# A selective-scan decoder block on one core: in the five quads without X tiles, TensorE sums the third sequence's shared products in a kept PSUM bank

## The chip, the cores and the metric

One NeuronCore of a Trainium2 chip runs the whole program. The metric is the device time of one execution in microseconds (us). The kernel before takes 2988.18 us, the median of 3 runs (2986.87 to 2988.26).

## What is computed

Input `x` is 16 sequences of 128 tokens and 1024 features, all float32. Three residual layers follow one another, each closed by a layer norm. Only the first matters here, a Mamba-like block:

```
proj = x @ W_in.T;  x, gate = proj[:, :2048], proj[:, 2048:]
x    = silu(causal_conv4(x))                      # u
ts, B, C = rms parts of x @ W_x.T                 # 64, 16, 16 columns
dt   = softplus(ts @ W_dt.T + b_dt);  A = -exp(A_log)
state[d, n] = state[d, n] * exp(dt[d] * A[d, n]) + dt[d] * u[d] * B[n]   # over time
y[d] = sum over n of state[d, n] * C[n]           # n = 0..15
out  = ((y + u * D) * silu(gate)) @ W_out.T
```

The sum over `n`, the 16 indices of the state, is what the change touches.

## The kernel before, in words

Tokens are cut into 4 groups of 4 sequences (512 tokens), the 2048 channels into 16 tiles of 128. A **quad** is 4 channel tiles of one group; 16 quads (s = 0 to 15, four to a group) run one after another, and each goes through the 16 indices n. One index of one quad is called a **step** below.

What a step does, engine by engine:

- ScalarE (ACT) writes exp(dt*A) of each of the 4 tiles into banks 0 and 1 (L1168).
- GpSimd (POOL) makes dt*u*B for all 4 tiles in one instruction (L1346).
- VectorE (DVE) scans each tile over time (L1433, 4 a step). It does so two steps ahead: during step n it scans for n+2.
- TensorE (PE) transposes the scanned states, so that tokens lie on partitions, one **turn** of 4 transposes for each sequence b = 0 to 3, into bank 2 (b even) or 3 (b odd) (L620). A turn waits until its bank has been read.
- The product with C[n] and the sum over n: sequences 0, 1 and 2 are done by DVE in one instruction each, `acc = bank * C + acc` (`dve_acc`, L1449, or L1445 for the first index). Sequence 3 (`OWN`) is multiplied by ACT (`act_part`, L912) and added by POOL (`pool_sums`, L1277). The third sequence, b = 2, called `SPLIT`, is divided: for the indices in `SHARED` = (0, 3, 6, 9, 12) ACT multiplies (`act_part2`, L926) and POOL adds into `acc2` (`pool_sums2`, L1285); for the other 11 DVE does it.

Between the turns PE works through **filler**: matmuls of 128x512 that make the Z tiles (gate, 8 products each, L526), the X tiles (conv input, 8 each, also L526), the D tiles (dt, 1 each, L538) and the O tiles (output projection of the quad before, 4 each, L550). `ORDER` fixes their order and `SIZES` how many come in the first and the second half of a step: turns 0 and 1, filler, turns 2 and 3, filler. X tiles are made ahead and are finished with quad 10 (`has_x`), so in quads 11 to 15 their places in the order are empty. Quads 11 and 15 are the last of their group and follow the fourth row of `ORDER`; 12, 13 and 14 follow the other.

At the end of a quad PE waits for the sums, turns them back (4 **Y** tiles, L661 to L664, where a matmul by the identity adds `acc2` to the third sequence), and DVE adds u*D (L1558) and multiplies by the gate (L1568, which counts up `fin`).

All X, Z, D, O and Y tiles live in banks 4 to 7, handed out in turn: `home` is bank 4 + k % 4 for the k-th of them, and `pe_room` waits until the tile four places earlier has been read (`FREED`).

Of the kernel before, what the change touches and what calls it, by code (L numbers as in the profile page):

```python
# [33 lines left out]
QD = 4  # L34
# [18 lines left out]
SPLIT = OWN - 1  # L53
SHARED = (0, 3, 6, 9, 12)
KEPT = OWN * N - len(SHARED)


LEAD = 5 * QD
EARLY = DT + 2
HEAD = 4  # L60
OPENING = "X-2 X-1 Z0 X0 D0 Z1 X1 D1 D2 Z2 D3 X2 Z3 X3".split()
# [34 lines left out]
def kept(s, n, b):  # L96

    return KEPT * s + OWN * n - sum(v < n for v in SHARED) + b + 1 - (b == SPLIT and n in SHARED)


def shared(s, n):

    return len(SHARED) * s + sum(v <= n for v in SHARED)

# [9 lines left out]
JOBS = jobs()  # L114
PLACE = {j: k for k, j in enumerate(JOBS)}
TILES = [j for j in JOBS if j[0] in "XZ"]
# [16 lines left out]
def program(nc, a, out):  # L133
# [4 lines left out]
    with ExitStack() as ctx:  # L138
# [100 lines left out]
        def home(kind, i):  # L239
            return bank(4 + PLACE[kind, i] % 4)  # L240

# [341 lines left out]
        def pe_filler(pe, s, p):  # L583
# [18 lines left out]
            assert start == sum(sizes)  # L602

        def pe_step(pe, s):
            g, q = divmod(s, NQ)
            for n in range(N):
                U = N * s + n

                def turn(b):

                    if b == 1:
                        after(pe, "part_ok", U)
                    elif b > 1:
                        pe.wait_ge(S["acc_ok"], kept(s, n, b - 2))
                    elif U and (n - 1) % N in SHARED:
# [37 lines left out]

            pe.wait_ge(S["acc_ok"], KEPT * (s + 1))
# [260 lines left out]
        def act_part2(act, s, n):  # L915

            k = SHARED.index(n)
            act.wait_ge(S["t_done"], QD * (N * s + n) + SPLIT + 1)
            if k == 0:
                after(act, "yt_mm", QD * s)  # L920
                act.wait_ge(S["cg_ok"], s // NQ + 1)
                dst = acc2
            else:
                after(act, "sum2_ok", (len(SHARED) - 1) * s + k - 2)
                dst = part2[:, k % 2, :]
# [3 lines left out]
        def act_opening(act, n, slot):  # L929
# [229 lines left out]
        def act_step(act, s):  # L1159
            q = s % NQ  # L1160
            for n in range(N):
# [10 lines left out]
                if U >= 2:  # L1172
                    if (U - 2) % N in SHARED:
                        act_part2(act, (U - 2) // N, (U - 2) % N)
                    act_part(act, (U - 2) // N, (U - 2) % N)

        def act_keys(act, b, o):
# [101 lines left out]
        def pool_sums2(pool, s, n):  # L1279
            k = SHARED.index(n)  # L1280
            if k == 0:
                return
            pool.wait_ge(S["part2_ok"], shared(s, n))
            after(pool, "sum2_ok", (len(SHARED) - 1) * s + k - 1)
            nc.gpsimd.tensor_tensor(acc2, acc2, part2[:, k % 2, :], ALU.add).then_inc(S["sum2_ok"], 1)  # L1285
# [18 lines left out]
        def pool_step(pool, s):  # L1304
# [9 lines left out]
            for n in range(N):  # L1314
# [121 lines left out]
        def dve_acc(dve, s, n, b):  # L1436
# [9 lines left out]
            else:  # L1446
                before = n - 2 if b == SPLIT and n - 1 in SHARED else n - 1
                dve.wait_ge(S["acc_ok"], kept(s, before, b))
# [84 lines left out]
        def dve_step(dve, s):  # L1533
            if s % NQ == 0:
                after(dve, "acc_ok", KEPT * s)
                after(dve, "part_ok", N * s)
                after(dve, "part2_ok", len(SHARED) * s)
                if s > 0:
                    dve_c(dve)
            for n in range(N):  # L1540
                U = N * s + n

                for part in range(2):
                    for b in range(2 * part, min(2 * part + 2, OWN)):
                        if b != SPLIT or n not in SHARED:
                            dve_acc(dve, s, n, b)
# [306 lines left out]
        def _(pool):  # L1853
# [138 lines left out]
```

## Time and profile before

| | |
|---|---|
| median of 3 runs | 2988.18 us |
| the profiled execution | 2988.28 us, its span 2986.3 us |
| busy PE / DVE / POOL / ACT | 2728.6 / 2563.8 / 1918.7 / 1694.1 us |
| quad 10, the last with X tiles | 126.4 us |
| quads 11, 12, 13, 14, 15 | 124.3, 118.5, 124.3, 118.2, 114.0 us |
| the rest after quad 15 | 774.6 us, which the change does not touch |

A quad is taken here from the last Y turn of one to the last Y turn of the next. The clock column of the windows view is the mean clock granted to TensorE, 1.00 being 2.4 GHz; the two levels are 1.2 and 2.4 GHz. A busy PE includes matmuls that overlap their neighbours, so start-to-start times are used for prices. Each float32 product of 128x512 is two MATMUL records, each transpose one.

### The profile page before, as it was taken

The numbers are of one execution on the slowest core, as the hardware profiler recorded it, in microseconds if no ns is written. First come the engines' busy times: TensorE is split into PE (matmuls) and PEld (weight loads), VectorE is DVE, ScalarE is ACT, GpSimd is POOL, SyncE is SP. The second block draws the span as 40 slices with busy tenths as digits, with TensorE's granted clock in tenths as the row PEclk, the third lists the DMA queues.
The fourth block names the chain that finished last, engine by engine and source line by source line (L and its number), as shares of the span: only waits on it lengthen the run. The fifth ranks groups of instructions, "written<-read, shape, count | busy, mean of one in ns | idle before, by whom it ended". The sixth has DMA issues, their size and how long they took to land.

```text
span 2986.3 us, 35300 instructions
## 1 busy us (share of the span) xinstructions
PE 2728.6 (91%) x11120; PEld 1559.2 (52%) x11120; DVE 2563.8 (86%) x3529; ACT 1694.1 (57%) x2848; POOL 1918.7 (64%) x885
## 2 busy tenths in 40 slices
PE   8978899999989999998999888788889999999996
PEld 4445555555555555555555455455544555555553
DVE  2389999999999999999999999999966787787785
ACT  2356566575656656565565655656534555555553
POOL 1159897888969888896988988889841222222221
PEclk9989899999999999999999999899999999999998
DMA  4443333534243343424333322322401211111110
GB/s 155 144 109 88 97 93 101 144 91 135 84 153 99 108 138 86 137 85 158 93 107 101 100 87 78 132 84 68 117 29 37 98 56 56 63 56 56 63 58 27
DMA packets 132876, 281.32 MB, mean 94 GB/s; under 512 B 12528, under 2 KB 12656, under 8 KB 132224
## 3 DMA queue, kind: packets, MB, share of 16 engines
q1 hardware_dynamic: 132736, 279.59, 31.3%
q8 instruction: 72, 1.18, 0.2%
q14 instruction: 68, 0.56, 0.1%
HBM read 245.86 MB, written 33.69 MB: 94 GB/s over the span
## 4 chain that ended last, share of the span: by engine, by line
PE 53%; DVE 32%; issue 8%; ACT 5%; DMA 1%; POOL 1%; DVEq 0%; SPq 0%; ACTq 0%; POOLq 0%
DVE arena L1433 17%; PE banks L526 14%; PE banks L550 9%; DVE arena L1449 7%; PE banks L620 7%; PE banks L766 4%; PE banks L719 3%; PE banks L675 3%; PE banks L700 3%; PE banks L563 2%; PE banks L730 2%; PE banks L690 2%; DVE arena L1378 2%; ACT banks L1168 1%; PE banks L773 1%
## 5 line engine op out<-in xcount | busy, mean ns | idle before, releaser
L1346 POOL TENSOR_TENSOR arena<-arena 128x2048 f32<-128x2048 f32 x254 | 1153.9, 4543 | 78.3 <-PE banks L620 78.3
L1433 DVE TENSOR_TENSOR_SCAN arena<-banks,arena 128x512 f32<-128x512 f32 x1024 | 1185.1, 1203 | 13.5 <-POOL arena L1346 7.5
L1168 ACT ACTIVATE banks<-arena,a_sb 128x508 f32<-128x508 f32 x1024 | 696.9, 684 | 734.5 <-DVE arena L1433 731.0
L526 PE MATMUL banks<-arena 128*128 128x512 f32 x2048 | 954.0, 603 | 11.5 <-DMA arena<-in_xT 8.2
L620 PEld LDWEIGHTS banks<-ident,arena 128*128 128x128 f32 x4096 | 492.6, 146 | 406.8 <-issue 176.6
L620 PE MATMUL banks<-ident,arena 128*128 128x128 f32 x4096 | 574.3, 284 | 127.9 <-DVE arena L1449 66.5
L526 PEld LDWEIGHTS banks<-arena 128*128 128x128 f32 x2048 | 373.1, 195 | 363.0 <-issue 358.2
L1449 DVE SCALAR_TENSOR_TENSOR arena<-banks,cg,arena 128x512 f32<-128x512 f32 x640 | 452.6, 737 | 74.9 <-PE banks L620 74.1
L550 PE MATMUL banks<-arena 128*128 128x512 f32 x1024 | 470.5, 598 | 5.5 <-DMA arena<-in_WoutT 4.2
L1277 POOL TENSOR_TENSOR arena<-arena 128x512 f32<-128x512 f32 x240 | 306.4, 1277 | 210.1 <-ACT arena L912 207.6
L1359 POOL TENSOR_TENSOR arena<-arena 128x512 f32<-128x512 f32 x128 | 141.3, 1104 | 433.0 <-DVE arena L1614 432.9
L550 PEld LDWEIGHTS banks<-arena 128*128 128x128 f32 x1024 | 185.9, 193 | 187.4 <-issue 185.2
L1378 DVE SCALAR_TENSOR_TENSOR arena<-banks,taps,arena 128x508 f32<-128x508 f32 (+2 forms) x192 | 141.6, 737 | 102.8 <-ACT arena L821 98.3
L912 ACT ACTIVATE arena<-banks,cg 128x512 f32<-128x512 f32 x256 | 171.9, 671 | 13.2 <-PE banks L620 13.2
L1200 ACT ACTIVATE arena<-arena 128x512 f32<-128x512 f32 x128 | 80.7, 630 | 172.2 <-DVE arena L1603 171.9
L1289 POOL TENSOR_TENSOR arena<-arena 128x512 f32<-128x512 f32 x64 | 81.9, 1280 | 133.2 <-ACT arena L835 133.2
L1599 DVE TENSOR_REDUCE arena<-banks 128x8 f32<-128x512 f32 x128 | 88.2, 689 | 87.8 <-PE banks L719 87.7
L719 PE MATMUL banks<-arena 128*128 128x512 f32 x256 | 131.7, 596 | 1.3 <-DVE rbuf L1462 1.3
L1368 POOL TENSOR_TENSOR ve<-ve,mhalf 128x1 f32<-128x1 f32 x32 | 17.4, 542 | 174.4 <-DVE ve L1646 174.4
L700 PE MATMUL banks<-arena 128*128 128x512 f32 x256 | 122.9, 592 | 0.0
L675 PE MATMUL banks<-arena 128*128 128x512 f32 x256 | 120.5, 593 | 1.7 <-ACT arena L1182 1.7
L766 PE MATMUL banks<-arena 128*128 128x512 f32 x256 | 115.1, 593 | 0.7 <-ACT arena L1208 0.7
(140 smaller groups left out, 2987.2 us busy)
## 6 DMA issues: line engine op xcount, KB each, us to landing
arena<-b_scratch SPq DMA_DIRECT2D x128, 512.0 KB, 5.2
arena<-in_WinX SPq DMA_DIRECT2D x128, 256.0 KB, 2.9
arena<-in_WinZ SPq DMA_DIRECT2D x128, 256.0 KB, 2.7
arena<-in_WoutT SPq DMA_DIRECT2D x32, 1024.0 KB, 5.8
u_scratch<-arena SPq DMA_DIRECT2D x64, 256.0 KB, 5.1
arena<-u_scratch SPq DMA_DIRECT2D x16, 1024.0 KB, 9.4
arena<-x_scratch SPq DMA_DIRECT2D x32, 512.0 KB, 3.5
arena<-in_xT SPq DMA_DIRECT2D x14, 1024.0 KB, 8.1
```

The source lines that it names most:

```text
L526: last = nc.tensor.matmul(home(kind, i), wr[w % 2][:, k, :], x[:, k, :], start=(k == 0), stop=(k == KC - 1))
L550: last = nc.tensor.matmul(home("O", i), yq[:, k, b * P:(b + 1) * P], w[:, k, :], start=(k == 0), stop=(k == QD - 1))
L620: last = nc.tensor.transpose(bank(2 + b % 2)[:, i * P:(i + 1) * P], hb[n % 4][:, i * GT + b * P:i * GT + (b + 1) * P], ident[:, :])
L675: last = nc.tensor.matmul(bank(2 + h), wk[:, o * P:(o + 1) * P], cn[:, h * HALF:(h + 1) * HALF], start=True, stop=True)
L700: last = nc.tensor.matmul(bank(6), cT[:, t, :], ekT[:, t, :], start=(t == 0), stop=(t == NT - 1))
L719: nc.tensor.matmul(bank(t % 2), x1[:, t * P:(t + 1) * P], wq, start=True, stop=True)\
L766: last = nc.tensor.matmul(bank(5 + 2 * h), mt[:, o, :], qs[:, o, h * HALF:(h + 1) * HALF], start=(o == 0), stop=(o == OT - 1))
L1168: nc.scalar.activation(by_seq(bank(i % 2))[:, :, 1:SEQ], by_seq(dt[s % 2][:, i, :])[:, :, 1:SEQ], ACT.Exp, scale=a_sb[:, QD * q + i, n:n + ...
L1277: nc.gpsimd.tensor_tensor(v, v, part[:, n % 2, :], ALU.add).then_inc(S["sum_ok"], 1)
L1346: nc.gpsimd.tensor_tensor(hb[n % 4].rearrange("p (i t) -> p i t", i=QD), dtu, brep[pair % 3][:, n % 2:n % 2 + 1, :].broadcast_to([P, QD, G ...
L1433: nc.vector.tensor_tensor_scan(h, bank(i % 2), h, 0.0, ALU.mult, ALU.add)\
L1449: last = nc.vector.scalar_tensor_tensor(acc[:, b, :], bank(2 + b % 2), c, acc[:, b, :], ALU.mult, ALU.add)
```

## The change

`BANKED` = 11. From quad 11 on three things differ:

- `SHARED` of these quads is (0, 2, 3, 5, 6, 7, 8, 9, 10, 12), ten indices in place of five. ACT makes all ten products into the two halves of `part2`, and none of them into `acc2`.
- POOL adds none of them. PE does: `pe_banked` multiplies `part2` by the identity into bank 7, which keeps the sum through the quad. Index n's comes in step n+1, after turns 2 and 3. At the end of the quad ACT copies bank 7 to `acc2` (`act_banked`), and the Y tiles are made as before.
- X, Z, D, O and Y tiles rotate over banks 4 to 6, three instead of four, so `pe_room` waits for the tile three places earlier.

```
+BANKED = (NG * DT - LEAD + QD - 1) // QD
+SHARED = [(0, 3, 6, 9, 12) if s < BANKED else (0, 2, 3, 5, 6, 7, 8, 9, 10, 12) for s in range(NS)]
...
+def places():
+
+    bank_of, last_of, last, quad = {}, {}, {}, 0
+    for k, (kind, i) in enumerate(JOBS):
+        quad = i // QD if kind == "Z" else quad
+        room = 4 if quad < BANKED else 3
+        bank_of[kind, i] = b = 4 + k % room
+        last_of[kind, i] = last.get(b)
+        last[b] = kind, i
+        if quad == BANKED - 1 and b == 7:
+            last_of["A"] = kind, i
+    return bank_of, last_of
...
         def home(kind, i):
-            return bank(4 + PLACE[kind, i] % 4)
+            return bank(PLACE[kind, i])
...
+        def pe_banked(pe, s, n):
+
+            k = SHARED[s].index(n)
+            if k == 0 and s == BANKED:
+                kind, i = LAST["A"]
+                pe.wait_ge(S[FREED[kind]], i + 1)
+            elif k == 0:
+                pe.wait_ge(S["pa_copied"], s - BANKED)
+            pe.wait_ge(S["part2_ok"], shared(s, n))
+            nc.tensor.matmul(bank(7), ident[:, :], part2[:, k % 2, :], start=(k == 0),
+                             stop=(k == len(SHARED[s]) - 1)).then_inc(S["pa_mm"], 1)
...
                 turn(2)
                 turn(3)
+                if s >= BANKED and n - 1 in SHARED[s]:
+                    pe_banked(pe, s, n - 1)
...
-            pe.wait_ge(S["sum2_ok"], (len(SHARED) - 1) * (s + 1))
+            if s < BANKED:
+                pe.wait_ge(S["sum2_ok"], LENT[s + 1] - s - 1)
+            else:
+                pe.wait_ge(S["pa_copied"], s - BANKED + 1)
...
         def act_part2(act, s, n):
...
-            if k == 0:
+            if s >= BANKED:
+                if s == BANKED:
+                    act.wait_ge(S["sum2_ok"], LENT[s] - s)
+                after(act, "pa_mm", LENT[s] - LENT[BANKED] + k - 1)
+                act.wait_ge(S["cg_ok"], s // NQ + 1)
+                dst = part2[:, k % 2, :]
+            elif k == 0:
...
+        def act_banked(act, s):
+
+            act.wait_ge(S["pa_mm"], LENT[s + 1] - LENT[BANKED])
+            act.wait_ge(S["yt_mm"], QD * s)
+            nc.scalar.activation(acc2, bank(7), ACT.Copy).then_inc(S["pa_copied"], 1)
...
         def pool_sums2(pool, s, n):
-            k = SHARED.index(n)
-            if k == 0:
+            k = SHARED[s].index(n)
+            if k == 0 or s >= BANKED:
                 return
```

PE in quad 12, from the second half of step 5 to the first turns of step 10. Before (L620 turns, L526 Z, L538 D, L550 O tiles; x8 is two turns):

```order
L620 MATMUL banks<-ident,arena 128x128 x8
L526 MATMUL banks<-arena 128x512 x4
L620 MATMUL banks<-ident,arena 128x128 x8
L526 MATMUL banks<-arena 128x512 x2
L620 MATMUL banks<-ident,arena 128x128 x8
L526 MATMUL banks<-arena 128x512 x2
L538 MATMUL banks<-tsb,wdt 128x512
L620 MATMUL banks<-ident,arena 128x128 x8
L550 MATMUL banks<-arena 128x512 x3
L620 MATMUL banks<-ident,arena 128x128 x8
L550 MATMUL banks<-arena 128x512 x4
```

Now, the same stretch (L650 turns, L544 Z, L556 D, L568 O tiles, L631 the new product):

```order
L650 MATMUL banks<-ident,arena 128x128 x8
L544 MATMUL banks<-arena 128x512 x4
L650 MATMUL banks<-ident,arena 128x128 x8
L544 MATMUL banks<-arena 128x512 x2
L650 MATMUL banks<-ident,arena 128x128 x8
L631 MATMUL banks<-arena,ident 128x512
L544 MATMUL banks<-arena 128x512 x2
L556 MATMUL banks<-tsb,wdt 128x512
L650 MATMUL banks<-ident,arena 128x128 x8
L568 MATMUL banks<-arena 128x512 x3
L650 MATMUL banks<-ident,arena 128x128 x8
L631 MATMUL banks<-arena,ident 128x512
```

One product is added after turns 2 and 3 of step 6 and of step 7, and likewise of 8, 9, 10, 11, 13, and of 1, 3 and 4; nothing else of the filler moved.

PE at the end of quad 12, the Y tiles and the next quad's first turn, with what each waits for. Before:

```order
L661 MATMUL banks<-ident,arena 128x128 [waits sum2_ok,r_added,sum_ok,acc_ok]
L661 MATMUL banks<-ident,arena 128x128 x2
L662 MATMUL banks<-ident,arena 128x128
L664 MATMUL banks<-ident,arena 128x128
...
L661 MATMUL banks<-ident,arena 128x128 [waits r_added]
L661 MATMUL banks<-ident,arena 128x128 x2
L662 MATMUL banks<-ident,arena 128x128
L664 MATMUL banks<-ident,arena 128x128
L620 MATMUL banks<-ident,arena 128x128 [waits acc_ok,scan_ok]
```

Now:

```order
L696 MATMUL banks<-ident,arena 128x128 [waits pa_copied,r_added,sum_ok,acc_ok]
L696 MATMUL banks<-ident,arena 128x128 x2
L697 MATMUL banks<-ident,arena 128x128
L699 MATMUL banks<-ident,arena 128x128
...
L696 MATMUL banks<-ident,arena 128x128 [waits fin]
L696 MATMUL banks<-ident,arena 128x128 x2
L697 MATMUL banks<-ident,arena 128x128
L699 MATMUL banks<-ident,arena 128x128
L650 MATMUL banks<-ident,arena 128x128 [waits acc_ok,scan_ok]
```

The fourth Y tile waits for `fin`, DVE's last reading of the first, where it waited for an O tile's reading (`r_added`).

## Rows read from the trace of the kernel before

**Rows 1.** The page: busy times (share of the span), and the chain by engine.

```profile
PE 2728.6 (91%) x11120; PEld 1559.2 (52%) x11120; DVE 2563.8 (86%) x3529; ACT 1694.1 (57%) x2848; POOL 1918.7 (64%) x885
...
PE 53%; DVE 32%; issue 8%; ACT 5%; DMA 1%; POOL 1%; DVEq 0%; SPq 0%; ACTq 0%; POOLq 0%
```

**Rows 2.** Windows: length, busy PE, PEld, DVE, ACT, POOL; clock, DMA.

```profile
1486.00:1612.40 126.40, 121.99 (x518) 70.94 (x518) 122.05 (x142) 78.67 (x129) 110.25 (x45) 1.00 0.33 102
1612.40:1736.70 124.30, 104.93 (x443) 63.12 (x441) 116.60 (x138) 73.38 (x128) 107.82 (x41) 0.93 0.31 100
1736.70:1855.20 118.50, 102.53 (x422) 61.67 (x421) 112.17 (x127) 70.09 (x113) 103.62 (x40) 0.90 0.27 79
...
1979.50:2097.70 118.20, 102.10 (x423) 61.48 (x422) 112.91 (x128) 70.10 (x113) 105.13 (x41) 0.90 0.27 79
2097.70:2211.70 114.00, 99.29 (x431) 59.70 (x430) 101.56 (x116) 57.81 (x93) 84.03 (x36) 0.93 0.29 71
```

**Rows 3.** Instruction groups of quad 12: count | busy, mean ns | idle before.

```profile
L1449 DVE SCALAR_TENSOR_TENSOR arena<-banks,cg,arena 128x512 f32<-128x512 f32 x40 | 28.3, 736 | 5.0 <-PE banks L620 4.8
L1277 POOL TENSOR_TENSOR arena<-arena 128x512 f32<-128x512 f32 x15 | 19.1, 1272 | 7.3 <-ACT arena L912 7.2
```

**Rows 4.** Timeline, DVE, quad 12, step 10: start, length.

```profile
1811.58 0.72 DVE L1449 SCALAR_TENSOR_TENSOR arena<-banks,cg,arena 128x512 f32<-128x512 f32 x1
1812.23 2.32 DVE L1433 TENSOR_TENSOR_SCAN arena<-banks,arena 128x512 f32<-128x512 f32 x2
```

**Rows 5.** Timeline, PE, quad 12, steps 7 to 11, some of its rows.

```profile
1785.83 2.74 PE L550 MATMUL banks<-arena 128*128 128x512 f32 x6
1788.40 1.04 PE L620 MATMUL banks<-ident,arena 128*128 128x128 f32 x8
...
1803.94 1.02 PE L538 MATMUL banks<-tsb,wdt 128*128 128x512 f32 x2
1806.16 1.15 PE L620 MATMUL banks<-ident,arena 128*128 128x128 f32 x8 [1.20 <-ACT arena L926]
...
1812.45 1.94 PE L620 MATMUL banks<-ident,arena 128*128 128x128 f32 x8 [1.67 <-DVE arena L1449]
1814.18 4.90 PE L526 MATMUL banks<-arena 128*128 128x512 f32 x6
1818.92 1.04 PE L620 MATMUL banks<-ident,arena 128*128 128x128 f32 x8
```

**Rows 6.** Timeline, PE, quad 12, steps 2 and 3.

```profile
1750.62 1.94 PE L620 MATMUL banks<-ident,arena 128*128 128x128 f32 x8 [2.32 <-DVE arena L1445]
1753.41 1.97 PE L620 MATMUL banks<-ident,arena 128*128 128x128 f32 x8 [0.85 <-DVE arena L1449]
...
1757.85 1.04 PE L620 MATMUL banks<-ident,arena 128*128 128x128 f32 x8
```

**Rows 7.** Timeline, ACT, quad 12, the shared product of step 12.

```profile
1827.56 0.69 ACT L1168 ACTIVATE banks<-arena,a_sb 128x508 f32<-128x508 f32 x1 [0.43 <-DVE arena L1433]
1828.18 0.67 ACT L926 ACTIVATE arena<-banks,cg 128x512 f32<-128x512 f32 x1
```

**Rows 8.** Timeline, PE, quad 12, the turns after it.

```profile
1829.00 3.62 PE L620 MATMUL banks<-ident,arena 128*128 128x128 f32 x16 [2.99 <-ACT arena L926]
```

**Rows 9.** Timeline, PE, quad 11, steps 13 and 14.

```profile
1708.89 1.02 PE L550 MATMUL banks<-arena 128*128 128x512 f32 x2
1711.38 1.26 PE L620 MATMUL banks<-ident,arena 128*128 128x128 f32 x8 [1.46 <-DVE arena L1449]
```

**Rows 10.** Waits, quads 11 to 15: who for whom, us in all, times, longest.

```profile
DVE arena L1433 <- POOL arena L1346: 5.1, 4, 3.4
```

**Rows 11.** Instruction groups of quads 11 to 15: the Y tiles' first turns.

```profile
L661 PE MATMUL banks<-ident,arena 128*128 128x128 f32 x60 | 10.7, 291 | 6.1 <-issue 6.1
```

**Rows 12.** Timeline at the end of quad 12: the fourth Y tile, and `fin` of the first.

```profile
1854.67 0.49 PE L661 MATMUL banks<-ident,arena 128*128 128x128 f32 x3
1854.76 0.68 DVE L1568 TENSOR_TENSOR arena<-banks,arena 128x512 f32<-128x512 f32 x1
```

More of the change, by code:

```diff
@@ L53 @@
 SPLIT = OWN - 1
-SHARED = (0, 3, 6, 9, 12)
-KEPT = OWN * N - len(SHARED)
 LEAD = 5 * QD
 EARLY = DT + 2
+BANKED = (NG * DT - LEAD + QD - 1) // QD
+SHARED = [(0, 3, 6, 9, 12) if s < BANKED else (0, 2, 3, 5, 6, 7, 8, 9, 10, 12) for s in range(NS)]
+KEPT = [OWN * N * s - sum(map(len, SHARED[:s])) for s in range(NS + 1)]
+LENT = [sum(map(len, SHARED[:s])) for s in range(NS + 1)]
 HEAD = 4
@@ L96, in kept @@
 def kept(s, n, b):
-    return KEPT * s + OWN * n - sum(v < n for v in SHARED) + b + 1 - (b == SPLIT and n in SHARED)
+    return KEPT[s] + OWN * n - sum(v < n for v in SHARED[s]) + b + 1 - (b == SPLIT and n in SHARED[s])
 def shared(s, n):
-    return len(SHARED) * s + sum(v <= n for v in SHARED)
+    return LENT[s] + sum(v <= n for v in SHARED[s])
 def jobs():
@@ L114 @@
 JOBS = jobs()
-PLACE = {j: k for k, j in enumerate(JOBS)}
+def places():
[9 more added lines that the diff above has]
+    return bank_of, last_of
+PLACE, LAST = places()
 TILES = [j for j in JOBS if j[0] in "XZ"]
@@ L614, in turn @@
                         pe.wait_ge(S["acc_ok"], kept(s, n, b - 2))
-                    elif U and (n - 1) % N in SHARED:
+                    elif U and (n - 1) % N in SHARED[(U - 1) // N]:
                         pe.wait_ge(S["part2_ok"], shared((U - 1) // N, (U - 1) % N))
@@ L923, in act_part2 @@
             else:
-                after(act, "sum2_ok", (len(SHARED) - 1) * s + k - 2)
+                after(act, "sum2_ok", LENT[s] - s + k - 2)
                 dst = part2[:, k % 2, :]
@@ L1172, in act_step @@
                 if U >= 2:
-                    if (U - 2) % N in SHARED:
+                    if (U - 2) % N in SHARED[(U - 2) // N]:
                         act_part2(act, (U - 2) // N, (U - 2) % N)
                     act_part(act, (U - 2) // N, (U - 2) % N)
+                if s >= BANKED and n == N - 1:
+                    act_banked(act, s)
         def act_keys(act, b, o):
@@ L1446, in dve_acc @@
             else:
-                before = n - 2 if b == SPLIT and n - 1 in SHARED else n - 1
+                before = n - 2 if b == SPLIT and n - 1 in SHARED[s] else n - 1
                 dve.wait_ge(S["acc_ok"], kept(s, before, b))
@@ L1534, in dve_step @@
             if s % NQ == 0:
-                after(dve, "acc_ok", KEPT * s)
+                after(dve, "acc_ok", KEPT[s])
                 after(dve, "part_ok", N * s)
-                after(dve, "part2_ok", len(SHARED) * s)
+                after(dve, "part2_ok", LENT[s])
                 if s > 0:
@@ L1544, in dve_step @@
                     for b in range(2 * part, min(2 * part + 2, OWN)):
-                        if b != SPLIT or n not in SHARED:
+                        if b != SPLIT or n not in SHARED[s]:
                             dve_acc(dve, s, n, b)
```

17 lines of the change are left out of this document (8 added, 9 removed).

## The prediction, made before the changed kernel was run

> **What bounds the kernel now.** I read the page first: TensorE is busy for 91% of the span, VectorE for 86%, and the chain that ends last lies 53% on the one and 32% on the other [rows 1]. That is a mean over the whole program, so the windows by quad come next, since only quads 11 to 15 change. Quad 10, with X tiles, has PE busy for 121.99 of 126.40 us at a clock of 1.00. In quad 12, PE is busy for 102.53 of 118.50 us at 0.90, DVE for 112.17; quad 14 is like it [rows 2]. So DVE looks like the bound of the late quads, with some 6 us of waits. The timeline shows it is not so simple. Filler is uneven: in steps 7, 8 and 9 of quad 12 PE works without one idle gap from 1785.83 to the end of the D product that starts at 1803.94, and has only 1.20 us before the turn at 1806.16 [rows 5]. There PE and DVE are both full. In light steps (2, 5, 10 to 13) PE waits 2.32 us for a sum of DVE, and the turn behind that gap is slow: 1.94 us for two turns, where 1.04 is the full-speed length [rows 5, 6]. GpSimd is the third bound, at the ends: DVE's scans wait for it four times, 5.1 us in all, the longest of 3.4 us in step 14 of quad 11 [rows 10], and the Y tiles of the five quads are idle for 6.1 us in all before they start, for its last sum [rows 11].
>
> **The change part by part.** The sum is made against the profiled execution, 2988.28 us (span 2986.3), 0.1 above the median.
>
> *DVE.* Each quad loses 5 instructions of 0.736 us busy [rows 3]. What one really takes is start to start, 1811.58 to 1812.23, or 0.65 us [rows 4]. Five quads save 25 x 0.65 = 16.3 us of DVE if DVE is what bounds those steps. New shared indices are 2, 5, 7, 8, 10.
>
> *PE.* Ten products of 128x512 are added to a quad. Three such products start 1785.83, and the next turn 1788.40: 2.57 / 3 = 0.86 us each [rows 5], 8.6 us a quad, 43 us in all. Those that come in light steps (1, 4, 10, 13) lie in waits. The others do not:
> - Steps 6 to 9 get four, 3.44 us. The slack was 1.20 us before the turn at 1806.16 [rows 5]. About 2.0 to 2.2 us are left on PE. DVE behind it has about 0.9 us of slack at step 10 (it still adds two O tiles there), so step 10 comes 1.0 to 1.4 us later, in place of 1.95 us earlier (indices 5, 7, 8).
> - Steps 3 and 11 get one each, in stretches in which DVE waits for PE: 0.7 to 0.86 each.
>
> *Handing over from ACT.* In a shared step the next turn waits for ACT's product. ACT starts its exp at 1827.56, the product at 1828.18 [rows 7], and the turn comes at 1829.00 [rows 8], 1.44 us after the exp could start. In an unshared step DVE's own sum stands there: from 1811.58 to the turn at 1812.45, 0.87 us [rows 4, 5]. Index 10 changes from the one to the other right before filler that bounds: +0.6. At 2, 5, 7, 8 PE is later anyway.
>
> *The clock.* The slow turn at 1812.45 and the three products behind it take until 1818.92, 6.47 us [rows 5]. At full speed they are 0.87 + 2.58 = 3.45, so 3.0 us are lost to the lower level in step 11 alone, and the 16 transposes from 1829.00, 3.62 us long, lose about 0.6 on the path [rows 8]. What raises the hope is quad 11: there a product at 1708.89 stands in the wait, the gap behind it is 1.46 us and not 2.32, and the two turns at 1711.38 take 1.26 us, nearly full speed [rows 9]. The change puts such a product into steps 1, 4, 10 and 13. Bounds for a quad are 0 (the clock falls as before) and -3.6 us (it never falls). I take half, since I cannot tell from the gaps alone which will do. The Trainium skill's page "TensorE: Matmul & The Clock Gate" says, in its Part 1, that the low clock is the default and activity releases it; by that rule the whole 3.6 us would come back. The same page, section "A second HAM failure mode: psum-queue depth-cycling", says that small idles between groups which rotate through PSUM banks make the clock oscillate; by that one nothing would. No row here says which holds for the changed order.
>
> *POOL.* Four additions of 1.27 us go from each quad [rows 3]; start to start they are 1.23. Two of them, indices 9 and 12, lie in the stretch before quad 11's wait of 3.4 us [rows 10], so its chain comes 2.4 us earlier. Of the 6.1 us before the Y tiles [rows 11], 2.6 are quad 11's, the other 3.5 lie in quads 12 to 14: I take 0.8 each in 12 and 14, and 2.5 in quad 13, which has most of the scans' other waits too (1.7 us in three) [rows 10].
>
> *Three banks.* The fourth Y tile now waits until DVE has multiplied the first by its gate. That instruction starts at 1854.76 and takes 0.68, so it ends at 1855.44; before, the fourth tile started at 1854.67 [rows 12]. With the handing over: +0.86 at each of four quad ends, where step 0 is PE-bound, and nothing at quad 15. Within a quad most tiles find the bank three back read long ago; the first O tile now waits for a D tile that DVE adds one step before: 0.2. ACT's copy of bank 7 (like its other copies, some 0.6 us) falls in step 15 and is hidden by ACT's waits.
>
> *Sum.* For quads 12 and 14: +0.8 (step 3), +1.2 (steps 6 to 9), +0.6 +0.86 (step 10, 11), +0.2, -0.8, +0.86 = +3.7 with the clock as it was, +0.1 with it kept, half-way +1.9 each. Quad 13: 1.7 less for POOL, so +0.2. Quad 11: -2.4 + 0.86 = -1.6; its own extra 0.9 is swallowed by the wait for POOL. Quad 15: +1.3 (steps 3 and 4) +1.46 (10, 11) - 1.3 (indices 7 and 8, where PE has room) = +1.5, less 1 for the clock. In all 3.8 + 0.2 - 1.6 + 0.5 = **+2.9 us** from the halves. The steps' small savings that I left at nothing pull the other way, and I round down: +2 us, 2990.
>
> **The rivals.**
> 1. *DVE's relief counts in full.* The 16.3 us come back, POOL's with them, and PE's products fit. For it: DVE is busy 112 of 118.5 us. Against: PE without a gap through steps 7 to 9. It would give 2988.3 - 16.3 = 2972. It decides if the turns of steps 8 to 10 come earlier than they did. 0.15.
> 2. *The clock is kept in every light step.* All else as in the sum: 0.1 x 2 - 1.6 x 2 - 0.5 = about -4, 2984. 0.15.
> 3. *PE's products in full, the clock as before* (slower). The place is steps 6 to 11, where turns are late and DVE waits; price +3.7 for quads 12 and 14, +2 for 13, -1.6 and +1.5: about +9, 2997.5. It decides once the clock of quads 12 to 14 stays at or under 0.92. 0.15.
> 4. *The three banks stall PE.* A tile in every quad waits for a read that comes a step late, 2 to 3 us before filler that bounds: +12 above the forecast, 3002. The order of PE shows such waits, on `dt_ok`, `z_exp`, `r_added`; by their places only one is close. 0.1.
>
> That the change does not do what it says gets no chance: PE's order has the products in place.
>
> **How the numbers follow.** The forecast, 2990, has 0.45, its own range 2984 to 2996. Measurement tells about 0.2% from no change, or 6 us: faster is under 2982.2, slower over 2994.2. Faster: 0.15 (rival 1) + 0.05 of rival 2 + 0.03 = 0.23. Slower: most of rivals 3 and 4 and an edge of the forecast, 0.29. The rest, 0.48, is within. The range leaves out rival 1 and reaches to rival 4: 2979 to 3002.
>
> **What would show it.** In the changed profile: DVE 3.7 us less busy in each of the five quads; ten more products; quads 12 and 14 at 118 to 121 us and quad 11 at 122 to 123; the clock of 12 to 14 at 0.93 to 0.97; turns of steps 8 to 10 later against their quad's start by 1 to 2 us; DVE's waits for PE grown; its wait of 3.4 us for POOL under 1.5 us; the fourth Y tile 0.8 us apart from the third. Quads under 116 us would prove me wrong, as would a clock that falls further.

## The result, and the profile after

The change makes the kernel 0.15% slower: 2993.66 us (median of 20 runs) against 2988.61 (20 runs of the kernel before beside them), ratio 1.0015, 95% interval 1.0008 to 1.0021. That is within the 0.2% taken as the bound of what can be told, and 3.7 us above the forecast.

The page of the changed kernel, busy times and chain, as [rows 1]:

```profile
PE 2753.2 (92%) x11220; PEld 1562.6 (52%) x11220; DVE 2548.3 (85%) x3504; ACT 1707.0 (57%) x2878; POOL 1894.5 (63%) x865
...
PE 56%; DVE 29%; issue 8%; ACT 4%; POOL 1%; DMA 1%; DVEq 0%; SPq 0%; ACTq 0%; POOLq 0%
```

VectorE lost its 25 instructions and 15.5 us, GpSimd 20 instructions and 24.2 us; TensorE has 50 more products (100 records). The chain moved from VectorE to TensorE by three points.

Its windows by quad (10 to 15), as [rows 2]:

```profile
1484.20:1610.60 126.40, 122.00 (x519) 70.94 (x518) 122.05 (x142) 78.68 (x129) 110.25 (x45) 1.00 0.32 101
1610.60:1733.50 122.90, 106.94 (x463) 61.89 (x462) 113.52 (x133) 76.01 (x134) 102.39 (x37) 0.99 0.33 102
1733.50:1854.50 121.00, 106.98 (x442) 60.84 (x441) 109.93 (x124) 72.63 (x119) 100.83 (x37) 0.96 0.24 78
1854.50:1978.90 124.40, 107.80 (x443) 63.12 (x441) 116.16 (x139) 76.94 (x123) 100.68 (x37) 0.95 0.37 112
1978.90:2100.10 121.20, 107.17 (x442) 61.05 (x441) 109.79 (x123) 72.71 (x119) 100.93 (x37) 0.96 0.27 79
2100.10:2216.90 116.80, 104.48 (x451) 61.14 (x450) 98.74 (x112) 60.39 (x99) 77.80 (x31) 0.97 0.25 73
```

The granted clock rose from 0.90 to 0.96 in quads 12 and 14, and yet these quads are 2.5 and 3.0 us longer. The five quads are 7.0 us longer together (599.3 to 606.3). The span grew by 5.9; the parts ahead of quad 11 and behind quad 15, whose code is the same, wander by some us from one profiled run to another (1609.9 to 1614.9 ahead of quad 11), so the experiments are read by the five quads beside the time. The quads are those of one profiled execution, the time is a median: the 20 executions of the change itself lie between 2987.82 and 2997.63 us.

Who waits for whom in quads 11 to 15, as [rows 10] (engine, line, waited for: us, times, longest; L1498 is DVE's sum, L650 a turn, L967 ACT's shared product, L1482 a scan, L1395 POOL's dt\*u\*B, L696 a Y tile, L1617 `fin`, L1326 POOL's own sum):

```profile
DVE arena L1498 <- PE banks L650: 48.3, 37, 3.0
...
PE banks L650 <- DVE arena L1498: 29.2, 33, 4.5
PE banks L650 <- ACT arena L967: 28.9, 14, 3.0
...
PE banks L696 <- DVE arena L1617: 3.3, 5, 0.7
...
PE banks L696 <- POOL arena L1326: 2.0, 1, 2.0
...
DVE arena L1482 <- POOL arena L1395: 1.4, 1, 1.4
```

The same view of the kernel before (its window begins at 1620, 8 us into quad 11):

```profile
PE banks L620 <- DVE arena L1449: 48.7, 39, 5.4
...
DVE arena L1449 <- PE banks L620: 23.9, 23, 3.0
...
PE banks L620 <- ACT arena L926: 21.0, 16, 3.0
```

VectorE has 15.5 us less to do and waits 24.4 us more for turns: what it saved, and more, became a wait for TensorE. Where, the ends of each step's last scan show. "Steps a to b" is the time from the end of the scans made in step a - 1 to the end of those made in step b, in us:

| | steps 0, 1 | 2 to 5 | 6 to 9 | 10 to 13 | 14, 15 |
|---|---|---|---|---|---|
| quad 12, before | 22.3 | 26.5 | 27.7 | 29.9 | 13.9 |
| quad 12, after | 21.5 | 27.7 | 29.3 | 29.6 | 13.9 |
| quad 14, before | 20.6 | 26.3 | 27.7 | 29.8 | 13.9 |
| quad 14, after | 20.7 | 27.8 | 29.3 | 29.6 | 13.9 |

Steps 2 to 5 and 6 to 9 lose 1.2 to 1.6 us each. Steps 10 to 13, where the clock was to be won, give back 0.2 to 0.3.

### The profile page after: what moved, and what is told of

It is laid out like the page before. It is cut to its first block, busy times and chain, and to the rows that moved or that the text cites. A ratio compares the mean times of both kernels' runs of the same rounds, so it can differ in the third digit from the quotient of the medians.

```text
span 2992.2 us, 35483 instructions
## 1 busy us (share of the span) xinstructions
PE 2753.2 (92%) x11220; PEld 1562.6 (52%) x11220; DVE 2548.3 (85%) x3504; ACT 1707.0 (57%) x2878; POOL 1894.5 (63%) x865
## 4 chain that ended last, share of the span: by engine, by line
PE 56%; DVE 29%; issue 8%; ACT 4%; POOL 1%; DMA 1%; DVEq 0%; SPq 0%; ACTq 0%; POOLq 0%
PE banks L544 15%; DVE arena L1482 15%; PE banks L568 9%; PE banks L650 7%; DVE arena L1498 6%; PE banks L801 4%; PE banks L754 4%; PE banks L710 3%; PE banks L735 3%; PE banks L581 2%; PE banks L765 2%; PE banks L725 2%; DVE arena L1427 1%; ACT banks L1215 1%; PE banks L808 1%
## 5 line engine op out<-in xcount | busy, mean ns | idle before, releaser
L1395 POOL TENSOR_TENSOR arena<-arena 128x2048 f32<-128x2048 f32 x254 | 1153.7, 4542 | 83.3 <-PE banks L650 83.3
L1482 DVE TENSOR_TENSOR_SCAN arena<-banks,arena 128x512 f32<-128x512 f32 x1024 | 1182.7, 1202 | 11.6 <-ACT banks L1215 5.6
L544 PE MATMUL banks<-arena 128*128 128x512 f32 x2048 | 950.0, 601 | 12.3 <-DMA arena<-in_xT 8.1
L650 PEld LDWEIGHTS banks<-ident,arena 128*128 128x128 f32 x4096 | 481.7, 143 | 395.2 <-issue 178.0
L650 PE MATMUL banks<-ident,arena 128*128 128x128 f32 x4096 | 560.8, 279 | 112.4 <-DVE arena L1498 47.9
L544 PEld LDWEIGHTS banks<-arena 128*128 128x128 f32 x2048 | 372.3, 194 | 370.0 <-issue 364.5
L1498 DVE SCALAR_TENSOR_TENSOR arena<-banks,cg,arena 128x512 f32<-128x512 f32 x615 | 434.3, 738 | 98.8 <-PE banks L650 98.0
L568 PE MATMUL banks<-arena 128*128 128x512 f32 x1024 | 471.2, 599 | 4.8 <-DMA arena<-in_WoutT 4.4
L1326 POOL TENSOR_TENSOR arena<-arena 128x512 f32<-128x512 f32 x240 | 306.4, 1277 | 233.0 <-ACT arena L947 226.4
L568 PEld LDWEIGHTS banks<-arena 128*128 128x128 f32 x1024 | 187.0, 193 | 194.2 <-issue 192.9
```

The costliest lines, as they stand in the source:

```text
L544: last = nc.tensor.matmul(home(kind, i), wr[w % 2][:, k, :], x[:, k, :], start=(k == 0), stop=(k == KC - 1))
L568: last = nc.tensor.matmul(home("O", i), yq[:, k, b * P:(b + 1) * P], w[:, k, :], start=(k == 0), stop=(k == QD - 1))
L650: last = nc.tensor.transpose(bank(2 + b % 2)[:, i * P:(i + 1) * P], hb[n % 4][:, i * GT + b * P:i * GT + (b + 1) * P], ident[:, :])
L1326: nc.gpsimd.tensor_tensor(v, v, part[:, n % 2, :], ALU.add).then_inc(S["sum_ok"], 1)
L1395: nc.gpsimd.tensor_tensor(hb[n % 4].rearrange("p (i t) -> p i t", i=QD), dtu, brep[pair % 3][:, n % 2:n % 2 + 1, :].broadcast_to([P, QD, G ...
L1482: nc.vector.tensor_tensor_scan(h, bank(i % 2), h, 0.0, ALU.mult, ALU.add)\
```

## The experiments

One question stood first: the change does three things (three banks in rotation, POOL's additions to PE, five more indices to ACT and PE), and the sum hides their signs. All runs at once, with the time (median), its ratio to the kernel before (95% interval) and the five quads of the profiled run in us; before has 2988.3 to 2989.2 us beside them and 599.3 in the quads. The intervals are about 0.1% wide to each side, or 3 us, so two times that differ by less than some 3 us are not told apart:

| run | what it is | time | ratio | quads |
|---|---|---|---|---|
| after | the change | 2993.66 | 1.0015 (1.0008 to 1.0021) | 606.3 |
| banks | three banks alone | 2992.02 | 1.0012 (1.0003 to 1.0021) | 605.0 |
| hot | banks, and idle products in the waits | 2985.91 | 0.9995 (0.9986 to 1.0004) | 602.0 |
| five | the change with the old five indices | 2980.87 | 0.9971 (0.9961 to 0.9981) | 594.2 |
| five_pool | five, POOL adds at 0, 3, 6, 9 | 2981.43 | 0.9980 (0.9971 to 0.9989) | 593.8 |
| five_pool12 | five, POOL adds at 3, 6, 9, 12 | 2988.80 | 1.0000 (0.9991 to 1.0009) | 602.3 |
| skip6 | the change, six of ten products left out | 2974.70 | 0.9953 (0.9939 to 0.9966) | 588.8 |
| no2_10 | the change without indices 2 and 10 | 2981.83 | 0.9977 (0.9968 to 0.9986) | 597.0 |
| y7 | the change, fourth Y tile in bank 7 | 2984.02 | 0.9988 (0.9979 to 0.9997) | 597.5 |
| five_y7 | five with that | 2976.66 | 0.9963 (0.9949 to 0.9977) | 590.0 |
| with2 | five_y7 and index 2 | 2984.13 | 0.9985 (0.9976 to 0.9994) | 594.1 |
| with10 | five_y7 and index 10 | 2979.18 | 0.9969 (0.9958 to 0.9981) | 590.3 |
| pick | five_y7 with 5, in quads 11 and 15 also 7 | 2978.02 | 0.9962 (0.9948 to 0.9976) | 588.2 |

### banks: the rotation over three banks alone

The kernel before with `places` of the change; nothing is banked.

```
-            return bank(4 + PLACE[kind, i] % 4)
+            return bank(PLACE[kind, i])
...
-            k = PLACE[kind, i]
-            if k >= 4:
-                kind, i = JOBS[k - 4]
+            if LAST[kind, i]:
+                kind, i = LAST[kind, i]
```

> The kernel before, with X, Z, D, O and Y tiles over three banks in quads 11 to 15 and nothing else; bank 7 lies idle. My account: the fourth Y tile waits for fin and costs 0.9 us a quad, the other waits by pe_room under 0.3; quad 12 from 118.5 to 119.5 us, in all +4.5 us (about 2993). Rival (three banks stall the filler): 2 to 3 us a quad, quad 12 over 121, in all +10 to +15, and then the bank rotation alone would be the change's whole loss.

It costs 3.6 us, and 5.7 in the five quads. PE waits for a bank in two places: the fourth Y tile (L674 here) for `fin` (L1581), 3.3 us in all, and filler, 1.9 us before Z tiles (L539) and 0.6 before O tiles (L563), where the kernel before has 0.0 before either. Of these, 0.9 is for `fin` and 1.5 for DVE's reading of a D tile (L1426). L1290 is POOL's own sum, for which the first Y tile waits as before:

```profile
L539 PE MATMUL banks<-arena 128*128 128x512 f32 x320 | 161.0, 639 | 1.9 <-DVE arena L1426 1.0 <-DVE arena L1581 0.9
L563 PE MATMUL banks<-arena 128*128 128x512 f32 x320 | 149.7, 606 | 0.6 <-DVE arena L1426 0.5
...
L674 PE MATMUL banks<-ident,arena 128*128 128x128 f32 x60 | 10.2, 279 | 9.4 <-POOL arena L1290 6.0 <-DVE arena L1581 3.3
```

Together that is 5.8 us, about what the quads grew by. Most of it is the fourth Y tile, 0.67 us in each of five quads; within the quads no wait for a bank is longer than 1.0 us. Windows of quads 12, 13 and 14:

```profile
1740.50:1860.30 119.80, 102.39 (x422) 60.02 (x422) 112.83 (x129) 70.03 (x113) 105.11 (x41) 0.91 0.27 81
1860.30:1985.50 125.20, 105.19 (x422) 62.99 (x422) 118.56 (x143) 74.39 (x117) 106.00 (x42) 0.86 0.35 110
1985.50:2104.50 119.00, 101.85 (x423) 60.83 (x422) 112.95 (x128) 70.15 (x113) 105.04 (x41) 0.91 0.26 81
```

The clock stays where it was, 0.91, but for quad 13, where it is 0.86 and was 0.92. So the rise to 0.96 does not come from the three banks; hot, below, tests whether products in the waits make it.

### five: the sum on PE, the indices as they were

```
-SHARED = [(0, 3, 6, 9, 12) if s < BANKED else (0, 2, 3, 5, 6, 7, 8, 9, 10, 12) for s in range(NS)]
+SHARED = [(0, 3, 6, 9, 12) if s < BANKED else (0, 3, 6, 9, 12) for s in range(NS)]
```

> The changed kernel with the old five shared indices (0, 3, 6, 9, 12), summed by TensorE. My account: four of its five products lie in light steps (1, 4, 10, 13), one in step 7 costs 0.9; the fourth Y tile +0.9; the clock kept and POOL relieved give back 2 to 3 us. Quad 12 at 117.5 to 118.5 us, in all -3 us against before (2985), so 8 us better than the change, though DVE does 25 instructions more. Rival (DVE's relief is what helps, and its five extra indices pay): slower than the change, 2996 or more.

It is 11.1 us faster than banks, and 12.8 faster than the change. Against the kernel before it gains 7.5 us, where I had expected 3. So one half of the change gains 11 us and the other, the five more indices, loses 13. PE in quad 12, steps 10 to 13, of banks (L633 turns, L539 Z tiles), then of five (L650, L544, L631 the product):

```profile
1813.61 1.78 PE L633 MATMUL banks<-ident,arena 128*128 128x128 f32 x8 [1.51 <-DVE arena L1462]
1817.24 1.94 PE L633 MATMUL banks<-ident,arena 128*128 128x128 f32 x8 [1.86 <-DVE arena L1462]
1818.97 3.73 PE L539 MATMUL banks<-arena 128*128 128x512 f32 x6
```

```profile
1807.65 1.31 PE L650 MATMUL banks<-ident,arena 128*128 128x128 f32 x8 [1.51 <-DVE arena L1498]
1808.80 1.02 PE L631 MATMUL banks<-arena,ident 128*128 128x512 f32 x2
1811.28 1.25 PE L650 MATMUL banks<-ident,arena 128*128 128x128 f32 x8 [1.46 <-DVE arena L1498]
1812.37 2.74 PE L544 MATMUL banks<-arena 128*128 128x512 f32 x6
```

From the first of these turns to the end of the three Z products there are 9.1 us in banks and 7.5 in five. One product of 0.86 us inside the wait leaves 1.46 us of idle time in place of 1.86, the two turns take 1.25 us, not 1.94, and the filler behind them is at full speed.

### hot: the same activity, no work

Banks, with two products of 128x256 from constants into the unused bank 7 in steps 1, 4, 10 and 13. The sum stays on POOL.

```
+                if s >= BANKED and n in (1, 4, 10, 13):
...
+                    for _ in range(2):
+                        nc.tensor.matmul(bank(7)[:, 0:DT * N], ident[:, :],
+                                         a_sb[:, :, :].rearrange("p d n -> p (d n)"), start=True, stop=True)
```

> The run banks (old five indices, POOL sums, three banks) with one product-sized piece of TensorE work whose result nobody reads, in steps 1, 4, 10 and 13 of quads 11 to 15. It adds 20 x 0.86 us of PE work and relieves no engine. My account (these pieces lie in light steps and keep the clock up): steps 11 and 12 of quads 12 and 14 from 15.1 to about 13 us, the clock of the quads from about 0.91 to 0.97, quads 11 to 15 together from 605.0 to 598 to 601 us. Rival (POOL's relief is what made the run five quick): the five quads stay at 605 or get longer.

6.1 us faster than banks by the medians, with nothing taken from any engine. In the five quads of the profiled runs it is 3.0 (605.0 to 602.0), less than I had expected (598 to 601). The same place:

```profile
1806.60 1.03 PE L660 MATMUL banks<-a_sb,ident 128*128 128x256 f32 x4
1809.09 1.25 PE L635 MATMUL banks<-ident,arena 128*128 128x128 f32 x8 [1.45 <-DVE arena L1471]
1810.18 2.74 PE L541 MATMUL banks<-arena 128*128 128x512 f32 x6
```

The same 1.25 and 2.74 as in five. Steps 11 and 12 of quad 14 go from 15.1 us in banks to 12.8 in both. By quad the clock of hot is 0.94, 0.97, 0.93, 0.93 and 0.93, where banks has 0.93, 0.91, 0.86, 0.91 and 0.91. So activity in a wait is enough to raise it. But in hot step 14 then grows from 6.7 to 8.4 us, in five to 7.2 only: something else comes up behind the clock.

### five_pool and five_pool12: which of POOL's additions counted

Both are five with four additions given back to POOL in each quad, their results not used, so that POOL's time changes. ACT, and in the second run POOL too, got waits that order the additions with the sum; in neither run does the view of waits show ACT waiting for an addition, or an addition waiting for TensorE.

```
+                if k < 4:
+                    pool.wait_ge(S["part2_ok"], shared(s, n))
+                    after(pool, "yt_mm", QD * s)
+                    after(pool, "sum2_ok", LENT[s] - s + k)
+                    nc.gpsimd.tensor_tensor(acc2, acc2, acc2, ALU.add).then_inc(S["sum2_ok"], 1)
```

and for the second, index 12 in place of index 0:

```
+            if k == 0:
+                return
...
+                spare = acc2 if k < 4 else part2[:, 1, :]
+                nc.gpsimd.tensor_tensor(spare, spare, spare, ALU.add).then_inc(S["sum2_ok"], 1)
```

> The run five with four additions of 128x512 a quad given back to POOL (at indices 0, 3, 6 and 9, on a buffer whose content is overwritten later), so that POOL works about as long as before. My account (the clock is most of it, POOL a part, chiefly in quad 11): the five quads from 594.2 to 597 to 599 us. Rival (POOL's relief is the gain): 603 to 605 us.

> This is the kernel of the run five with POOL's four additions given back at indices 3, 6, 9 and 12 in the five quads; index 12's sits at its old place on POOL, and all four results are overwritten, so that they cost time on POOL alone. The run five_pool gave POOL additions at 0, 3, 6 and 9 and cost nothing. My account: the addition of index 12 stands on POOL ahead of what the scans of step 14 wait for, which is what the run hot still pays against five; step 14 of quads 12 and 14 goes from 7.2 to 7.9 us up to 8.4 to 9.1, the step of 13 does not give it back, and the five quads last 597 to 602 us together against 594.2 of five; time 2984 to 2987 us. The rival: POOL's additions cost nothing anywhere, and what hot pays is something else (DVE's share of its sum); five quads 594, time 2981 us.

The additions at 0, 3, 6 and 9 cost nothing (593.8 us against 594.2), though I had expected 3 to 5 us. With the one of index 12 the quads take 602.3 us, and the time is 7.4 us longer than five_pool's. POOL and DVE in quad 12 of five_pool12 (L1339 is the added instruction, L1404 dt\*u\*B, L1491 the scans):

```profile
1830.17 1.27 POOL L1327 TENSOR_TENSOR arena<-arena 128x512 f32<-128x512 f32 x1
1831.41 1.04 POOL L1339 TENSOR_TENSOR arena<-arena 128x512 f32<-128x512 f32 x1
1832.41 4.52 POOL L1404 TENSOR_TENSOR arena<-arena 128x2048 f32<-128x2048 f32 x1
```

```profile
1836.96 2.34 DVE L1491 TENSOR_TENSOR_SCAN arena<-banks,arena 128x512 f32<-128x512 f32 x2 [1.67 <-POOL arena L1404]
```

The addition stands right before the instruction for which the scans wait. Of the five quads, its waits and those of five:

```profile
PE banks L696 <- POOL arena L1327: 7.4, 4, 2.6
DVE arena L1491 <- POOL arena L1404: 6.8, 4, 2.3
```

```profile
PE banks L696 <- POOL arena L1326: 4.5, 3, 1.7
DVE arena L1482 <- POOL arena L1395: 3.4, 3, 1.3
```

The two waits grow by 2.9 and 3.4 us. So twenty additions are gone in the change, and five of them carry what POOL's relief is worth, 7.4 us by the time and 8.5 by the quads once TensorE makes the sum. Some of it is the clock again, which is 0.93 in quad 12 of five_pool12 and 0.97 in five_pool.

### skip6: what PE's products cost

```
+            if n in (2, 5, 6, 7, 8, 10):
+                pe.sem_inc(S["pa_mm"], 1)
+                return
```

> The changed kernel with TensorE leaving out the six products of indices 2, 5, 6, 7, 8 and 10 (they are missing from the sum; ACT still makes them, DVE is still relieved). My account: PE is no longer full in steps 3, 6 to 9 and 11, so DVE's relief shows: quad 12 from 121.0 to 116.7 us, quad 14 alike, in all about -16 us against the change (2978). Rival (the hand-over from ACT or the banks are what costs): quad 12 stays above 119.5.

The sum lacks these six indices; all else is as in the change. 30 products fewer in the five quads: 606.3 - 588.8 = 17.5 us, or 0.58 us each, of the 0.86 that one takes. Steps 6 to 9 of quad 14 go from 29.3 to 27.5 us (four products, 0.45 each), step 9 from 7.76 to 6.37. TensorE is what bounds there. Skip6 is also 5.4 us shorter in the quads than five (588.8 to 594.2). Five has the five products of index 6, which at 0.58 us each are some 3 us of that. So with the products gone VectorE's relief is a gain after all, by my estimate of 2 to 3 us with the hand-overs from ACT in it; the products take more than that away.

### no2_10, with2, with10: which indices

```
+SHARED = [(0, 3, 6, 9, 12) if s < BANKED else (0, 3, 5, 6, 7, 8, 9, 12) for s in range(NS)]
```

and, on five_y7 (below), `(0, 2, 3, 6, 9, 12)` and `(0, 3, 6, 9, 10, 12)`.

> The changed kernel without indices 2 and 10 in its shared list (eight indices; DVE does these two again). My account after the step table: the loss sits behind indices 2 and 10, where a hand-over from ACT and a product stand right before filler that bounds, not in steps 6 to 9. Five quads from 606.3 to 594 to 597 us. Rival (my prediction's largest item, the four products in steps 6 to 9): 602 or more, since those four stay.

> The run five_y7 with index 2 shared as well. My account: step 2 is 0.65 shorter, steps 3 and 4 of quads 12 and 14 together 1.5 to 3 us longer (13.2 to 14.7 or 16.2); the five quads from 590.0 to 595 to 600 us. Rival: 590 or less.

> The run five_y7 with index 10 shared as well. It relieves DVE by 5 instructions (3.3 us) and adds 5 products (4.3 us) and a hand-over from ACT before step 11's filler. My account: step 10 is 0.65 shorter, steps 11 and 12 of quads 12 and 14 together 1.5 us longer (12.8 to 14.3) where the clock holds, 3.4 longer where it falls; the five quads from 590.0 to 595 to 600 us. Rival (the list of ten fails only as a whole, one more index alone pays): 590 or less.

Without 2 and 10 the quads take 597.0 us: these two carry 9.3 of the 12.1 us between five and the change, the other three 2.8 together. Added to five_y7 alone, index 2 costs 4.1 us in the quads and 7.5 in time. In quad 14 step 2 falls from 6.43 to 5.78 us, and step 4 rises from 7.44 to 9.28: the sum taken from DVE is repaid two steps later, behind the new product. Index 10 alone costs 0.3 in the quads and 2.5 in time, which can't be told from nothing and is far under the 5 to 10 us that I had expected: steps 11 and 12 of quad 14 rise by 1.7 us (12.80 to 14.49), but step 10 falls by 0.7 and step 14, which had waited for POOL, by 1.4. A step that comes later finds POOL done: of five_y7's 4.0 us of the scans' waits for POOL none is left in with10.

What index 10 costs depends on the clock behind it. PE in quad 12 of the change, in quad 13 of the same execution, and in quad 12 of with10:

```profile
1812.67 1.14 PE L650 MATMUL banks<-ident,arena 128*128 128x128 f32 x8 [2.14 <-ACT arena L967]
1813.65 4.44 PE L544 MATMUL banks<-arena 128*128 128x512 f32 x6
1817.93 1.04 PE L650 MATMUL banks<-ident,arena 128*128 128x128 f32 x8
```

```profile
1938.51 1.14 PE L650 MATMUL banks<-ident,arena 128*128 128x128 f32 x8 [2.14 <-ACT arena L967]
1939.49 2.74 PE L544 MATMUL banks<-arena 128*128 128x512 f32 x6
```

```profile
1807.20 1.15 PE L654 MATMUL banks<-ident,arena 128*128 128x128 f32 x8 [2.14 <-ACT arena L971]
1808.18 2.74 PE L548 MATMUL banks<-arena 128*128 128x512 f32 x6
1810.76 1.04 PE L654 MATMUL banks<-ident,arena 128*128 128x128 f32 x8
```

The turn waits for ACT's product, 2.14 us where five has 1.46 for DVE's sum. Behind that gap the three products take 4.44 us in quads 12 and 14 of the change and 2.74 in its quad 13; with10 has 2.74 in quads 12 and 14 and 4.03 in quad 13. So both occur in one kernel and one execution. Steps 11 and 12 together take 14.5 us where the products take 2.74 and 16.2 where they take 4.44.

### y7 and five_y7: the fourth Y tile out of the rotation

Bank 7 is free between ACT's copy and the next quad's first product, so the fourth Y tile can go there.

```
+        if quad >= BANKED and kind == "Y" and i % QD == QD - 1:
+            bank_of[kind, i], last_of[kind, i] = 7, None
+            continue
...
-                pe.wait_ge(S["pa_copied"], s - BANKED)
+                pe.wait_ge(S["fin"], QD * s)
```

> The changed kernel with the fourth Y tile of quads 11 to 15 in bank 7, which is free there between ACT's copy and the next quad's first product; the other tiles keep three banks. My account: the wait of PE for DVE before that tile (0.67 us idle, 0.86 in time) goes at each quad end: each quad 0.8 to 0.9 shorter, in all -4 us against the change (2989). Rival (PE's lateness there is hidden): no quad moves by more than 0.3.

> Five indices summed by TensorE, and the fourth Y tile in bank 7. Both gains add up, if they are of different places: 594.2 - 5 x 0.86 = 590 us for the five quads, about 2977 in time. Rival (the Y gain is hidden by POOL's last sum when DVE is not relieved): 593 or more.

On five it gains 4.2 us both in time and in the quads, about what banks lost. On the change it gains 9.6 in time and 8.8 in the quads, more than the wait is worth. The rest lies where the clock is higher: in the first window below (quad 12) it is 0.99, where the change has 0.96, and in the second (quad 13) 0.95, like the change.

```profile
1732.20:1849.90 117.70, 104.03 (x442) 59.67 (x441) 109.80 (x124) 72.52 (x119) 100.20 (x37) 0.99 0.26 78
1849.90:1975.80 125.90, 108.28 (x443) 62.51 (x442) 116.28 (x139) 76.88 (x123) 101.95 (x38) 0.95 0.36 109
```

```profile
1810.29 1.15 PE L654 MATMUL banks<-ident,arena 128*128 128x128 f32 x8 [2.14 <-ACT arena L971]
1811.28 2.74 PE L548 MATMUL banks<-arena 128*128 128x512 f32 x6
```

Same order, same gap of 2.14 us as in quad 12 of the change, and full speed. In quad 13 of y7 it is the other way round: 4.44 us behind the gap, where the change has 2.74, and the quad is 1.5 us longer. The quads 12 and 14 (117.7 us each) show what the lower clock costs the change: steps 2 to 5 take 26.7 us (27.7 and 27.8 in the change), steps 10 to 13 27.9 (29.6). The gain also differs between executions of y7: seven of its eleven last 2982.6 to 2985.0 us, the profiled one (2982.81) among them, and four 2987.4 to 2989.4.

So with the fourth Y tile in bank 7 the five more indices cost 7.4 us (2976.66 to 2984.02), not 12.8.

### pick: two more indices where they had done no harm

Five_y7 with the indices that the other runs left unharmed.

```
+SHARED = [(0, 3, 6, 9, 12) if s < BANKED else (0, 3, 5, 6, 7, 9, 12) if s % NQ == NQ - 1 else (0, 3, 5, 6, 9, 12)
+          for s in range(NS)]
```

> The run five_y7 with index 5 shared too, and in the two last quads of a group (11 and 15) index 7 as well. These stand where the step table shows DVE's relief and no later loss. My account: 0.65 less in step 5 of each quad, up to 0.7 given back in steps 8 and 9 of quads 12 to 14, 1 us less in step 7 of quads 11 and 15: the five quads from 590.0 to 586 to 589 us, time 2973 to 2976. Rival (any further product in the filled steps costs its 0.86): 591 or more.

588.2 us in the quads is the least of all versions that compute everything, but the time, 2978.02, is outside the 2973 to 2976 that I had expected and can't be told from five_y7's 2976.66. Five_y7 is 0.37% faster than the kernel before. The simpler one, five_y7, is the one to keep.

## Why the prediction was right, and where its steps were not

It was right that the change is within 0.2% of the kernel before, and the time lies in the forecast's own range. It was right as a balance of large terms of both signs, of which several were off; that they cancelled to within 3.7 us is in part luck.

- **VectorE's relief is not what counts.** Right. 15.5 us of busy time were taken from it, and its waits for turns grew by 24.4. Rival 1 falls.
- **TensorE in quads 12 and 14.** Steps 6 to 9: booked +1.2, measured +1.6. Steps 2 to 5: booked 0.8 for step 3 and 0.2 for the O tile's bank, measured +1.2 and +1.5. There I had laid the product of step 4 into a wait. It does lie in one (1766.80 in quad 12 of the change, with 1.46 us left behind it), but TensorE came to that wait later by the product of index 2. The clock is in it too, which I had priced in steps 11 and 12 only: behind the gap of 1.54 us before step 3's filler two products take 3.62 us (1751.93 in quad 12), and where they take 2.52 (quad 12 of y7) steps 2 to 5 are back at 26.7 us.
- **The clock.** The bounds held, 0.96 and 0.95 against the 0.93 to 0.97 that I named, and the sign of the cause is shown by hot: activity in a wait is enough. The step "I take half" was too much for quads 12 and 14, by 0.6 and 1.1 us, and stood on no row. It is not that every light step wins half: with five products the waits keep the clock nearly whole (0.96 to 0.97 in all five quads of five), and index 10, which I priced at +0.6 for the handing over, lengthens the gap and can lose it again in that very place. The rest of the sum for these quads holds: it had +0.1 with the clock kept, or -0.8 without the fourth Y tile's 0.86, and y7, whose clock is 0.99 there, has -0.8 and -0.5 (117.7 us against 118.5 and 118.2). The rule of the Trainium skill's page "TensorE: Matmul & The Clock Gate", Part 1, that activity releases the clock, agrees with hot (1.25 and 2.74 us behind the idle products). The same page of the Trainium skill says, in its section "A second HAM failure mode: psum-queue depth-cycling", that short idle times between groups which cycle through PSUM banks let the clock oscillate. The traces agree in so far as the clock is between its two levels in the mean of a quad, 0.90 with four banks in rotation and 0.91 with three in quads 12 and 14; but that nothing would come back, as I had worked out from it, is refuted by hot and five (0.97 in quad 12).
- **GpSimd.** Both waits shrank as said: the scans' from 5.1 to 1.4 us, the Y tiles' from 6.1 to 2.0. That the Y tiles' wait is for POOL's sum was my reading, since [rows 11] name no engine; the views of banks and of the change do name it. But I spread the value by counting additions (two of 1.2 us in quad 11) and by waits (0.8, 2.5 and 0.8 in quads 12 to 14). Five_pool and five_pool12 show that it all hangs on index 12's. With TensorE making the sum it is worth 8.5 us in the five quads, 0.8, 2.4, 1.9, 2.5 and 0.9 of them by quad, not the 2.4 + 1.6 + 2.5 that I booked (6.5).
- **Three banks.** Booked +0.86 at four quad ends and 0.2 in each of three quads, 4.0 in all; measured +3.6 in time and +5.7 in the quads, of it 0.67 us of idle at each of five quad ends and 2.5 before filler. Rival 4 had 12 and falls.
- **Quad by quad.** Quad 11: -1.4 (booked -1.6), the right sum by luck. GpSimd's part is there, -2.0 us in steps 14 and 15. But step 2 gains 2.2 us (9.3 to 7.1) that I had not booked, and hot, with idle products alone, has 1.5 of it (7.8): behind the product of step 1 its 16 small matmuls take 2.0 us, not 2.9. And steps 6 to 9 lose 2.2 us (26.4 to 28.5), where I had 0.9 and called it swallowed. Quad 13: +0.1 (booked +0.2). Quads 12 and 14: +2.5 and +3.0 (booked +1.9). Quad 15: +2.8 (booked +0.5), the largest miss. There I took 1.3 us off for indices 7 and 8 and 1 for the clock. Its steps 6 to 9 fell by 0.1 (25.02 to 24.95), and steps 10 to 13 rose by 1.9 (26.14 to 28.06). Only 0.4 of that comes with the full clock (26.51 in y7); the rest is two turns (1.94 us, 1.14 in y7) and two products (2.68, 1.88 in y7) at the lower level.
- **Slips in the working.** They change no reading: quad 11 is -2.4 + 0.86 = -1.5, not -1.6, and rival 2 adds up to -3.5, not -4. Rival 1's 2972 leaves out the GpSimd part that it names. And the wait of 2.32 us that I gave for every light step is 1.67 in step 11 of quad 12, before the turn at 1812.45 [rows 5].
- **Rivals 2 and 3.** The clock was kept more than in rival 3 and less than in rival 2, and the quads (+7.0) stand between my forecast (+2.9) and rival 3 (+9).

So the account by the times is: three banks +3.6 us, the sum moved to TensorE -11.1, five more indices +12.8. Of the 11.1, hot has 6.1 for the clock in the waits, and 5.0 are left for GpSimd; by the quads of the profiled runs it is 3.0 and 7.8, so the division is known no better than that. Of the 12.8, some 5 are absent with the fourth Y tile in bank 7 (7.4 from five_y7 to y7); the lower clock of quads 12, 14 and 15 in the change is where they lie, by the windows and steps above. Of my sum of +2.9 the three banks were 4.0 and all the rest -1.1; measured in time, the rest is +1.4 (5.05 - 3.6).

**What stays open:** why the same order with the same gap of 2.14 us is followed by products at the lower clock in quads 12 and 14 of the change and in quad 13 of y7 and with10, and at the full clock in the other of these quads. It is no property of the kernel, and each kernel has one profile, so how often either comes is not known. What comes earlier in the quad was not varied for it.

## What to carry to other kernels

Take a change of several parts apart before weighing it: here one part gained 11 us, another lost 13, and the sum looked like nothing. Before work is moved off an engine, ask which single instruction of it stands before a wait: one addition in four was worth all of POOL's relief, and VectorE's 25 instructions gained less than the products that replaced them cost TensorE. And a bank that rotates less costs where its last reader is late, so the tile that waits can be put into the kept bank while that one is idle.

## What the hardware showed unexpectedly

- Work in a wait raises TensorE's clock even when it computes nothing of use: from 0.91 to 0.97 in quad 12 of hot against banks, from 0.91 to 0.93 in quads 14 and 15, and 6.1 us in time.
- A gap of 2.14 us, with the same instructions around it, was followed by three products of 4.44 us in quads 12 and 14 and of 2.74 us in quad 13 of one execution, and the other way round in y7. A gain or loss of some 1.7 us at such a place is not a property of the order alone, and one profile of a kernel does not tell which it has in its other executions.
